# Fillers, moved steps, and the shared item and the product with V between the two banks of scores of a slot

## The chip, the cores and the metric

The kernel runs on one core of one Trainium2 chip. The metric is the device time of one execution in microseconds.

## What is computed

The input is X, 8 batches of 512 rows of 256 numbers in float32. After a layer norm, xn goes two ways: through causal attention with 16 heads of 16 and rotary positions, and through a linear layer whose input and weight are each rounded to fp8 (e4m3) with one scale for the whole tensor. Both results are added to X.

```python
Q, K, V = xn @ W_q.T, xn @ W_k.T, xn @ W_v.T           # split into 16 heads of 16
scores = rope(Q) @ rope(K).T * 16 ** -0.5              # causal: later keys masked
heads  = softmax(scores) @ V
attn   = heads_side_by_side @ W_o.T
ffn    = fake_quant_fp8(xn) @ fake_quant_fp8(weight).T + bias
out    = X + attn + ffn
# fake_quant_fp8(t): scale = 448 / max|t|; round(t * scale to e4m3) / scale
```

## The kernel before

All work is written out by hand, engine by engine, as one loop over slots (`for slot in range(FIRST_SLOT, END_SLOT)`, slots -11 to 162) in each of the five programs. Twenty slots (`SLOTS`) make a batch of 512 rows; slot 20n + s of batch n handles unit s of its exponents, while the row maxima of the same kind of unit run ten slots ahead (`LEAD`).

In a slot TensorE computes two halves of scores (`scores`, `attend`, `compare`). A half is one bank of transposed scores for the exponent (`st_ps`, two banks, heads of one half of the rows of the array) and one bank of plain scores for the row maximum (`s_ps`, three banks). `attend` waits until the exponent two banks before has been read (`exp_done`), `compare` until the row maximum three banks before has (`max_done`). ScalarE turns each `st_ps` bank into `prob` (`exp`), GpSimd masks it (`mask`), VectorE takes the row maxima (`row_max`).

After the scores TensorE does the slot's shared item, if it has one, in one of two banks `m_ps` that the items take by turns: a projection of Q or K (`qk`, read by VectorE's `rope`), of V (`v`, read by ScalarE's `copy_v` in the slot after), a turn of the row maxima (`mt`, read by VectorE's `split_max`, whose result goes by DMA into the rows of Q), a turn of the heads (`o`, read by VectorE's `norm`), a turn of the normed attention (`at`, read by ScalarE's `copy_at`), an output block (`fin`, read by VectorE's `finish`), and the two steps that spread the largest values for the fp8 scales (`spread`). `OFFSETS`, `LAST_FINS`, `EARLY` and `SPREAD` give the slots, `bank_free` waits for the reader of the item two before. Last in the slot comes the product with V (`pv`, into the one bank `o_ps`, 17 columns a head): for each group g of four heads its first block, 8 products, in slot 5g + 3 and the others, 24 products, in slot 5g + 6. The first block waits for the copy of the group before out of `o_ps` (`copy_heads`, ScalarE); the turn of heads frees `heads` for the next batch's copy.

Each engine's list of a slot, in order:

- ScalarE: `high_x` (every 20 slots), the two exponents (`exp`), `copy_turned` and `normalise` for the later batches' inputs, `copy_v`, at slot 21 the scaled weights, `qv` (scaled x for fp8), `copy_heads` of the last group (slot 22, that is 2 of the next batch), `copy_at`, `copy_heads` of the other groups (slots 7, 12, 17), `high` (half-precision part of Q and K, slots 16 and 1).
- VectorE: two banks of row maxima, `largest` (largest value of one batch, slots 0, 2, ... 14), the weight steps, `statistics` of batches 6 and 7 (slot -9), the readers of the items, the fp8 steps `qe` and `qc`.
- GpSimd: `split_x`, `mask`, `invert` of late batches, `rotate` and `low` for Q and K, the fp8 steps, the residual with the bias (`residual_at`).
- SP: all DMAs, in one list: residuals, rows of maxima, writing and reading back the split Q and K.

Ahead of the loop the inputs are normalised, batch 0 is projected (`project_whole`) and TensorE multiplies the identity by itself (`keep_busy`) between waits. In slots -10 to -3 it also turns the inputs of batches 2 to 7 (`turn_rows`).

Of the kernel before, what the change touches and what calls it, by code (L numbers as in the profile page):

```python
# [12 lines left out]
ALU = mybir.AluOpType  # L13
# [3 lines left out]
P = 128  # L17
# [37 lines left out]
LAST_FINS = {("fin", 0): 29, ("fin", 1): 30, ("fin", 2): 34, ("fin", 3): 35}  # L55
SPREAD = [(17, "spread", 0, 0), (19, "spread", 0, 1)]
# [7 lines left out]
TURN_SLOT = {2: -10, 3: -8, 4: -7, 5: -6, 6: -4, 7: -3}  # L64
DVE_STATS, ACT_STATS = (0, 1, 2, 3, 6, 7), (4, 5)


def schedule():
# [6 lines left out]
    items += [(slot, len(order), kind, n, k) for slot, kind, n, k in SPREAD]  # L75
    return [(slot, kind, n, k) for slot, _, kind, n, k in sorted(items) if n < NB - 1 or kind not in ("o", "at", "fin")]
# [39 lines left out]
def residual_at(slot, loop, last):  # L116

    for n in range(NB):
        if slot == SLOTS * n + (loop if n < NB - 1 else last):
            return n  # L120
    return None
# [5 lines left out]
def quant_at(slot, step):  # L127

    k = QUANT_STEPS.index(step)
    first, last, loop = (24, 25, 26, 27, 29), (8, 9, 12, 13, 15), (11, 13, 14, 24, 26)  # L130
    return [n for n in range(NB) if SLOTS * n + (first if n == 0 else last if n == NB - 1 else loop)[k] == slot]
# [17 lines left out]
def attention_ffn_block(nc, x, wq, wk, wv, wo, wf, bias, cos, sin, out):  # L149
    with ExitStack() as ctx:  # L150
# [303 lines left out]
        def _(eng):  # L454
# [81 lines left out]
            for slot in range(FIRST_SLOT, END_SLOT):  # L536
# [9 lines left out]
                if slot == -LEAD + 2:  # L546
                    invert(6)
                    invert(7)
# [4 lines left out]
                if slot == 23:  # L553
# [13 lines left out]
                n = residual_at(slot, 31, 17)  # L567
# [7 lines left out]
        def _(eng):  # L575
# [33 lines left out]
            def weight_step(s):  # L609
# [6 lines left out]
                if s == 15:  # L616
# [3 lines left out]
                if s == 17:  # L620
# [4 lines left out]
                    eng.tensor_scalar(amax_d[:, :], ident[0:2, 0:2], amax_r[:, 0:1], None, ALU.mult)\  # L625
                       .then_inc(wquant, 1)
                if s == 19:
# [5 lines left out]
                    eng.tensor_scalar(unscale[:, :], amax_b[:, :], 1.0 / FP8_MAX, None, ALU.mult).then_inc(wquant, 1)  # L633
                    eng.wait_ge(wquant, 5)
                    eng.tensor_scalar(scale[:, :], inv[:, :], FP8_MAX, None, ALU.mult).then_inc(wquant, 1)
# [3 lines left out]
                if s == 22:  # L639
# [100 lines left out]
            for slot in range(FIRST_SLOT, END_SLOT):  # L740
# [5 lines left out]
                if slot in range(0, 2 * NB, 2):  # L746
                    largest(slot // 2)
                weight_step(slot)
                if slot == -LEAD + 1:
                    statistics(6, 7)  # L750
# [17 lines left out]
        def _(eng):  # L768
# [96 lines left out]
            for slot in range(FIRST_SLOT, END_SLOT):  # L865
# [6 lines left out]
                if n is not None:  # L872
                    high_x(n)
                at = exponent_slot(slot)
# [6 lines left out]
                for n, i in [(n, i) for _, n, i in shared_at(slot - 1, "v")]:  # L881
                    copy_v(n, i, shared["v", n, i])
                if slot == 21:
                    eng.wait_ge(wquant, 7)
                    eng.mul(qv[:, 0:nw], wf_sb[:, :, :].rearrange("p c n -> p (c n)"), scale[:, 1:2])\
                       .then_inc(wf_scaled, 1)
                    eng.mul(wo_sb[:, :, :], wo_sb[:, :, :], scale[:, 0:1]).then_inc(wo_scaled, 1)
# [9 lines left out]
                n = batch_at(slot, 22)  # L897
                if n is not None:
                    copy_heads(n, NG - 1)
# [15 lines left out]
        def _(eng):  # L915
            eng.wait_ge(consts, 6)

            def keep_busy(count):

                for _ in range(count):  # L920
                    eng.matmul(s_ps[2][:, 0:P], ident[:, :], ident[:, :], start=True, stop=True)  # L921
# [68 lines left out]
            def scores(at, ahead):  # L990


                for half in range(2):
                    for i in range(2):
                        if at is not None and i < len(unit_parts(at[1] % 5, half)):
                            attend(*at, half, i)
                        if ahead is not None and i < len(MAX_BANKS[(2 * ahead[1] + half) % len(MAX_BANKS)]):
                            compare(ahead[0], 2 * ahead[1] + half, i)
# [89 lines left out]
            def bank_free(item):  # L1088
# [3 lines left out]
                if at >= 2:  # L1092
# [3 lines left out]
                    else:  # L1096
# [19 lines left out]
            keep_busy(24)  # L1116
# [65 lines left out]
```

## Time and profile before

| | us |
|---|---|
| time, median of 3 runs | 442.33 |
| lowest and highest of them | 439.71, 443.72 |
| the profiled execution | 441.93 |
| its span in the profile | 440.2 |
| TensorE busy | 392.0 |
| VectorE busy | 355.9 |
| ScalarE busy | 300.0 |
| GpSimd busy | 247.5 |

Busy time counts an engine's instructions with overlaps taken out once. A matmul's end is modelled, so a busy TensorE need not run at its peak. The granted clock is the share of full speed that TensorE was given; it has two levels here, 0.5 (1.2 GHz) and 1.0 (2.4 GHz).

### The profile page before, as it was taken

What the parts mean: (1) busy time and instruction counts of PE and PEld (TensorE: products, weight loads), DVE (VectorE), ACT (ScalarE), POOL (GpSimd) and SP (SyncE); (2) the same over time, 40 slices, a digit from 0 to 9 for tenths busy, and PEclk for the clock granted to TensorE, in tenths of its full rate; (3) what the DMA queues carried; (4) which work ended last, traced back from release to release, by engine and by line L of the source; (5) the groups of instructions that cost most, each with busy time, mean ns of one, the idle gap of its engine ahead of it and who ended that gap; (6) DMA issues with size and microseconds to landing.
All of it is one profiled execution on the core that took longest, in us unless ns stands there. A gap on an engine that the chain in (4) does not pass through costs nothing.

```text
span 440.2 us, 9436 instructions
## 1 busy us (share of the span) xinstructions
PE 392.0 (89%) x2986; PEld 206.8 (47%) x2986; DVE 355.9 (81%) x1360; ACT 300.0 (68%) x505; POOL 247.5 (56%) x270
## 2 busy tenths in 40 slices
PE   7997988989669999899989998999899988985976
PEld 6684652434224545454445444544454443442325
DVE  4869749798886999799979997999799978992104
ACT  3697736456566778677867786778677777765451
POOL 5555502343366857775777577757676745364360
PEclk9999575698578999999999999999999999999689
DMA  8962223000421115412441234123413431110111
GB/s 280 305 167 49 85 85 74 1 3 1 133 85 39 37 47 137 123 37 59 126 120 39 73 110 122 38 87 109 109 38 100 109 95 39 49 36 18 48 50 48
DMA packets 27810, 36.40 MB, mean 83 GB/s; under 512 B 3984, under 2 KB 25872, under 8 KB 26320
## 3 DMA queue, kind: packets, MB, share of 16 engines
q1 hardware_dynamic: 27760, 35.79, 28.9%
q8 instruction: 24, 0.39, 0.4%
q14 instruction: 26, 0.21, 0.2%
HBM read 22.94 MB, written 12.58 MB: 81 GB/s over the span
## 4 chain that ended last, share of the span: by engine, by line
PE 64%; DVE 17%; ACT 7%; issue 7%; POOL 2%; DMA 1%; DVEq 0%; ACTq 0%; POOLq 0%
PE o_ps L1075 15%; PE st_ps L965 10%; PE m_ps L1006 8%; DVE scratch L658 7%; PE m_ps L949 7%; PE s_ps L984 7%; PE m_ps L1033 7%; ACT prob L818 5%; DVE prod L606 3%; PE m_ps L1013 2%; PE s_ps L921 2%; PE m_ps L1041 1%; DVE prod L605 1%; PE m_ps L1053 1%; PE st_ps L929 1%
## 5 line engine op out<-in xcount | busy, mean ns | idle before, releaser
L818 ACT ACTIVATE prob<-st_ps,exp_scale 128x512 f32<-128x512 f32 x320 | 204.5, 688 | 96.6 <-PE st_ps L965 95.7
L658 DVE CUSTOM_DVE_ANT_0 scratch<-s_ps,causal 128x512 bf16<-128x512 f32 (+3 forms) x512 | 220.9, 483 | 34.2 <-PE s_ps L984 33.2
L511 POOL TENSOR_SCALAR_AFFINE_SELECT prob<-prob 128x512 f32<-128x512 f32 (+1 forms) x160 | 88.0, 551 | 156.0 <-ACT prob L818 154.2
L984 PE MATMUL s_ps<-k_st,q_st 48*128 48x512 f16 (+3 forms) x512 | 112.2, 319 | 13.2 <-DVE rowmax L658 13.1
L965 PE MATMUL st_ps<-q_st,k_st 50*128 50x128 f16 (+3 forms) x512 | 110.4, 316 | 12.6 <-ACT prob L818 11.0
L1075 PE MATMUL o_ps<-prob,v_sb 128*17 128x512 f32 (+3 forms) x1024 | 90.6, 476 | 6.9 <-ACT heads L832 5.1
L965 PEld LDWEIGHTS st_ps<-q_st,k_st 50*128 50x128 f16 x512 | 34.7, 96 | 98.2 <-ACT prob L818 71.2
L984 PEld LDWEIGHTS s_ps<-k_st,q_st 48*128 48x128 f16 x512 | 34.4, 96 | 30.4 <-DVE rowmax L658 22.0
L658 DVE DVE_READ_ACCUMULATOR2_ANT rowmax<- 128x1 f32 x512 | 41.0, 80 | 0.0
L1075 PEld LDWEIGHTS o_ps<-prob,v_sb 128*17 128x17 f32 x1024 | 24.4, 102 | 34.6 <-issue 20.3
L1006 PE MATMUL m_ps<-wv_sb,xnT 128*128 128x256 f32 x128 | 34.8, 419 | 0.0
L1033 PE MATMUL m_ps<-wo_sb,attnT 128*128 128x256 f32 x116 | 32.7, 404 | 0.0
L346 POOL TENSOR_TENSOR parts<-rot,parts 128x1024 f16<-128x1024 f32 x14 | 30.1, 2152 | 4.5 <-ACT parts L803 4.5
L1006 PEld LDWEIGHTS m_ps<-wv_sb,xnT 128*128 128x128 f32 x128 | 24.7, 203 | 7.2 <-issue 4.1
L605 DVE SCALAR_TENSOR_TENSOR prod<-m_ps,qk_scale,cos_sb 128x512 f32<-128x512 f32 x30 | 22.3, 742 | 7.0 <-PE m_ps L949 5.2
L679 DVE SCALAR_TENSOR_TENSOR x_res<-m_ps,both,x_res 128x256 f32<-128x256 f32 x29 | 13.9, 479 | 17.2 <-PE m_ps L1041 10.0
L832 ACT COPY heads<-o_ps 128x512 f32<-128x512 f32 x32 | 18.8, 588 | 11.7 <-PE m_ps L1013 8.3
L949 PE MATMUL m_ps<-x_parts,wk_parts 128*128 128x512 f32 x84 | 23.4, 413 | 0.0
L1033 PEld LDWEIGHTS m_ps<-wo_sb,attnT 128*128 128x128 f32 x116 | 19.6, 189 | 7.7 <-issue 6.2
L949 PE MATMUL m_ps<-x_parts,wq_parts 128*128 128x512 f32 x84 | 22.9, 410 | 0.0
L1013 PE MATMUL m_ps<-ident,heads 128*128 128x128 f32 x116 | 19.5, 292 | 3.5 <-DVE attn L671 3.4
L606 DVE SCALAR_TENSOR_TENSOR prod<-m_ps,qk_scale,sin_sb 128x512 f32<-128x512 f32 x30 | 22.1, 736 | 0.0
(123 smaller groups left out, 497.3 us busy)
## 6 DMA issues: line engine op xcount, KB each, us to landing
qk_parts<-parts SPq DMA_DIRECT2D x14, 512.0 KB, 3.1
xnT<-x_dram SPq DMA_DIRECT2D x8, 512.0 KB, 8.4
x_res<-x_dram SPq DMA_DIRECT2D x8, 512.0 KB, 5.1
q_st<-qk_parts SPq DMA_DIRECT2D x15, 256.0 KB, 4.5
k_st<-qk_parts SPq DMA_DIRECT2D x15, 256.0 KB, 3.7
out_dram<-x_res SPq DMA_DIRECT2D x7, 512.0 KB, 3.7
q_st<-qk_parts SPq DMA_DIRECT2D x17, 128.0 KB, 3.6
k_st<-qk_parts SPq DMA_DIRECT2D x17, 128.0 KB, 4.1
```

The source lines that it names most:

```text
L346: eng.tensor_tensor(parts[:, w, 1, a:z, :], rot[:, w, a:z], parts[:, w, 0, a:z, :], ALU.subtract).then_inc(low_done[w], z - a)
L511: eng.affine_select(out=ap, in_=ap, compare_op=ALU.is_ge, fill=0.0, base=0, pattern=pat, channel_multiplier=-1).then_inc(masked, 1)
L606: eng.scalar_tensor_tensor(out=c, in0=bank[:, :], scalar=to_range, in1=sin_sb[:, :], op0=ALU.mult, op1=ALU.mult)\
L658: eng.tensor_tensor_reduce(scratch[:, at % 3, col:col + w], s_ps[at % 3][:, col:col + w], causal[:, T - w:T], 1.0, NEG, ALU.add, ALU.max, ...
L818: eng.activation(prob[u][:, half * T:(half + 1) * T], st_ps[ST_BANK[2 * s + half]][:, :], ACT.Exp, scale=exp_scale[:, 0:1]).then_inc(exp_d ...
L949: mm = eng.matmul(bank[:, :], w_parts[k // 2][:, wp, c, k % 2, :], x_parts[:, xp, c, :], start=(i == 0), stop=(i == len(terms) - 1))
L965: mm = eng.matmul(st_ps[ST_BANK[i]][:, col:col + T - kb * P], k_rows(n, h, ROWS + SHIFT, slice(kb * P, (kb + 1) * P)), q_rows(n, h, ROWS + ...
L984: mm = eng.matmul(s_ps[(BANKS * n + f) % 3][:, col:col + (qb + 1) * P], q_rows(n, h, ROWS, slice(qb * P, (qb + 1) * P)), k_rows(n, h, ROWS ...
L1006: mm = eng.matmul(bank[:, t * D:(t + 1) * D], xnT[:, n, c, (2 * i + t) * P:(2 * i + t + 1) * P], wv_sb[:, c, :], start=(c == 0), stop=(c = ...
L1013: mm = eng.transpose(bank[:, g * P:(g + 1) * P], heads[:, g, qb * P:(qb + 1) * P], ident[:, :])
L1033: mm = eng.matmul(bank[:, 0:D], attnT[:, qb, c, :], wo_sb[:, c, :], start=(first and c == 0), stop=(not first and c == NC - 1))
L1075: mm = eng.matmul(o_ps[32 * i:32 * i + VW, kb * P:T], v_sb[:, n % 2, kb, g * HG + i, :], prob[u][:, col:col + T - kb * P], start=(kb == 0) ...
```

## The change

The diff does these things:

- TensorE: the two halves of scores are called apart. The first half, then `turn_rows`, fillers, the shared item and the product with V, then the second half.
- Fillers: 6 products of the identity in each of slots -10 to -1 (`FILL`, into `st_ps[1]`), and 8 in each of slots 0, 2, 4, 5, 7, 20, 22, 25 (`BUSY`), which take a turn among the shared items' banks. A wait for the weights' range (`w_max_done`) comes ahead of the loop, as `st_ps[1]` was read for it.
- ScalarE: `copy_heads` of the last group and `copy_v` come ahead of the slot's exponents. The other copies of heads stay behind them.
- VectorE: `largest` in slots 0, 2, 4, 5, 7, 8, 9, 11; `statistics` of batch 6 in slot -10, of 7 in slot -7; the weight steps one or two slots earlier; three operations on a few numbers in another form (`amax_d`, `unscale`, `scale`).
- GpSimd: `invert` of batch 6 in slot -9 and of 7 in -6; the weight's last fp8 steps a slot earlier; the residual of batch 6 in slot 148 instead of 151.
- The first two output blocks of batch 6 in slots 151 and 152 instead of 149 and 150; batch 0's fp8 steps a slot later; the two spread steps two slots earlier.

```diff
-LAST_FINS = {("fin", 0): 29, ("fin", 1): 30, ("fin", 2): 34, ("fin", 3): 35}
-SPREAD = [(17, "spread", 0, 0), (19, "spread", 0, 1)]
+LAST_FINS = {("fin", 0): 31, ("fin", 1): 32, ("fin", 2): 34, ("fin", 3): 35}
+SPREAD = [(15, "spread", 0, 0), (17, "spread", 0, 1)]
...
+FILL = {slot: 6 for slot in range(-LEAD, 0)}
+BUSY = {slot: 8 for slot in (0, 2, 4, 5, 7, 20, 22, 25)}
+LARGEST_SLOT = (0, 2, 4, 5, 7, 8, 9, 11)
...
+    items += [(slot, len(order), "busy", slot, count) for slot, count in BUSY.items()]
...
-def residual_at(slot, loop, last):
+def residual_at(slot, loop, last, last_but_one=None):
...
-        if slot == SLOTS * n + (loop if n < NB - 1 else last):
+        if slot == SLOTS * n + (last if n == NB - 1 else last_but_one or loop if n == NB - 2 else loop):
...
-    first, last, loop = (24, 25, 26, 27, 29), (8, 9, 12, 13, 15), (11, 13, 14, 24, 26)
+    first, last, loop = (25, 26, 27, 28, 30), (8, 9, 12, 13, 15), (11, 13, 14, 24, 26)
...
-                if slot == -LEAD + 2:
+                if slot == -LEAD + 1:
                     invert(6)
+                if slot == -LEAD + 4:
                     invert(7)
...
-                if slot == 23:
+                if slot == 22:
                     eng.wait_ge(wquant, 8)
...
-                n = residual_at(slot, 31, 17)
+                n = residual_at(slot, 31, 17, 28)
...
-                if s == 15:
+                if s == 13:
                     eng.wait_ge(amax_done, NB + 1)
...
-                if s == 17:
+                if s == 15:
...
-                    eng.tensor_scalar(amax_d[:, :], ident[0:2, 0:2], amax_r[:, 0:1], None, ALU.mult)\
+                    eng.tensor_tensor(amax_d[:, :], ident[0:2, 0:2], amax_r[:, 0:1].to_broadcast([2, 2]), ALU.mult)\
                        .then_inc(wquant, 1)
-                if s == 19:
+                if s == 17:
...
-                    eng.tensor_scalar(unscale[:, :], amax_b[:, :], 1.0 / FP8_MAX, None, ALU.mult).then_inc(wquant, 1)
+                    eng.tensor_scalar(unscale[:, :], shared["spread", 0, 1][:, 0:2], 1e-12, 1.0 / FP8_MAX, ALU.max, ALU.mult)\
+                       .then_inc(wquant, 1)
...
-                    eng.tensor_scalar(scale[:, :], inv[:, :], FP8_MAX, None, ALU.mult).then_inc(wquant, 1)
+                    eng.scalar_tensor_tensor(out=scale[:, :], in0=inv[:, :], scalar=FP8_MAX, in1=inv[:, :], op0=ALU.mult,
+                                             op1=ALU.max).then_inc(wquant, 1)
...
-                if s == 22:
+                if s == 21:
...
-                if slot in range(0, 2 * NB, 2):
-                    largest(slot // 2)
+                if slot in LARGEST_SLOT:
+                    largest(LARGEST_SLOT.index(slot))
                 weight_step(slot)
-                if slot == -LEAD + 1:
-                    statistics(6, 7)
+                if slot in (-LEAD, -LEAD + 3):
+                    statistics(6 if slot == -LEAD else 7)
...
+                n = batch_at(slot, 22)
+                if n is not None:
+                    copy_heads(n, NG - 1)
+                for n, i in [(n, i) for _, n, i in shared_at(slot - 1, "v")]:
+                    copy_v(n, i, shared["v", n, i])
                 at = exponent_slot(slot)
                 if at is not None:
                     exp(*at)
...
-                for n, i in [(n, i) for _, n, i in shared_at(slot - 1, "v")]:
-                    copy_v(n, i, shared["v", n, i])
-                if slot == 21:
+                if slot == 19:
...
+                if slot == 20:
                     eng.mul(wo_sb[:, :, :], wo_sb[:, :, :], scale[:, 0:1]).then_inc(wo_scaled, 1)
...
-                n = batch_at(slot, 22)
-                if n is not None:
-                    copy_heads(n, NG - 1)
...
-            def keep_busy(count):
+            def keep_busy(count, bank=s_ps[2]):
...
-                    eng.matmul(s_ps[2][:, 0:P], ident[:, :], ident[:, :], start=True, stop=True)
+                    eng.matmul(bank[:, 0:P], ident[:, :], ident[:, :], start=True, stop=True)
...
-            def scores(at, ahead):
-
-
-                for half in range(2):
-                    for i in range(2):
...
+            def scores(at, ahead, half):
+
+
+                for i in range(2):
...
-                    else:
+                    elif kind != "busy":
...
+            eng.wait_ge(w_max_done, 4)
...
-                scores(exponent_slot(slot), maximum_slot(slot))
+                scores(exponent_slot(slot), maximum_slot(slot), 0)
                 for n in [n for n, at_slot in TURN_SLOT.items() if at_slot == slot]:
                     turn_rows(n)
-                for item in shared_at(slot, *do):
+                if slot in FILL:
+                    keep_busy(FILL[slot], st_ps[1])
+                for item in shared_at(slot, "busy", *do):
                     bank_free(item)
+                    if item[0] == "busy":
+                        keep_busy(item[2], shared[item])
+                        continue
                     do[item[0]](item[1], item[2], shared[item]).then_inc(full[item[0]], 1)
...
+                scores(exponent_slot(slot), maximum_slot(slot), 1)
```

## Rows read from the trace of the kernel before

**Rows 1.** The page's first part: busy us (share of the span) xinstructions.

```profile
PE 392.0 (89%) x2986; PEld 206.8 (47%) x2986; DVE 355.9 (81%) x1360; ACT 300.0 (68%) x505; POOL 247.5 (56%) x270
```

**Rows 2.** Busy time by stretch; columns: stretch, us, busy per engine, PEclk, DMA, GB/s.

```profile
33.90:63.00 29.10, 26.61 (x110) 16.64 (x109) 21.67 (x93) 17.04 (x32) 12.38 (x12) 0.71 0.29 79
...
63.60:116.40 52.80, 43.58 (x284) 17.97 (x282) 48.28 (x162) 32.50 (x52) 20.15 (x27) 0.76 0.18 44
116.40:165.30 48.90, 42.84 (x328) 20.25 (x328) 41.55 (x161) 33.80 (x54) 30.51 (x32) 0.87 0.18 48
165.30:208.70 43.40, 41.24 (x349) 21.44 (x349) 40.36 (x159) 32.94 (x53) 29.48 (x31) 1.00 0.32 87
```

**Rows 3.** The same view of three stretches at the lower clock.

```profile
43.70:60.80 17.10, 17.01 (x61) 10.50 (x61) 10.40 (x44) 9.22 (x18) 6.87 (x5) 0.50 0.36 109
67.60:84.70 17.10, 15.25 (x88) 4.16 (x89) 15.74 (x56) 9.91 (x17) 6.29 (x8) 0.50 0.24 48
...
405.60:415.80 10.20, 8.73 (x49) 2.86 (x49) 2.54 (x6) 3.50 (x6) 3.41 (x4) 0.50 0.16 52
```

**Rows 4.** Timeline, slots 40 and 50 to 51: start us, us, engine line op out<-in.

```profile
165.22 1.13 PE L1033 MATMUL m_ps<-wo_sb,attnT 128*128 128x256 f32 x4
166.50 0.39 PE L965 MATMUL st_ps<-q_st,k_st 50*128 50x512 f16 x1
...
185.70 0.39 PE L965 MATMUL st_ps<-q_st,k_st 50*128 50x512 f16 x1
186.19 1.27 ACT L818 ACTIVATE prob<-st_ps,exp_scale 128x512 f32<-128x512 f32 x2 [1.20 <-PE st_ps L965]
186.24 1.67 PE L949 MATMUL m_ps<-x_parts,wq_parts 128*128 128x512 f32 x6
186.34 0.69 DVE L658 CUSTOM_DVE_ANT_0 scratch<-s_ps,causal 128x512 bf16<-128x512 f32 x1 [1.03 <-PE s_ps L984]
188.59 1.49 PE L1075 MATMUL o_ps<-prob,v_sb 128*17 128x384 f32 x24
```

**Rows 5.** Timeline of ScalarE in slots 41 and 42.

```profile
168.14 1.04 ACT L803 CAST parts<-rot 128x1024 f16<-128x1024 f32 x1
169.15 1.27 ACT L818 ACTIVATE prob<-st_ps,exp_scale 128x512 f32<-128x512 f32 x2
170.31 0.59 ACT L832 COPY heads<-o_ps 128x512 f32<-128x512 f32 x1
```

**Rows 6.** Timeline of TensorE in slot 48, the wait before each in brackets.

```profile
180.86 0.66 PE L1013 MATMUL m_ps<-ident,heads 128*128 128x128 f32 x4 [0.49 <-DVE attn L671]
...
182.25 1.05 PE L1075 MATMUL o_ps<-prob,v_sb 128*17 128x512 f32 x8 [0.73 <-ACT heads L832]
```

**Rows 7.** Timeline of slots 51 to 53.

```profile
189.49 1.15 ACT L895 ACTIVATE qv<-xnT,scale 128x1024 f32<-128x1024 f32 x1
...
191.67 0.60 ACT L832 COPY heads<-o_ps 128x512 f32<-128x512 f32 x1
...
193.26 1.05 PE L1075 MATMUL o_ps<-prob,v_sb 128*17 128x512 f32 x8
```

**Rows 8.** Timeline ahead of the loop: 24 fillers, two records each.

```profile
25.60 5.62 PE L921 MATMUL s_ps<-ident 128*128 128x128 f32 x48 [0.68 <-DVE parts L346]
```

**Rows 9.** Timeline of the weight steps in slots 17 and 19, and GpSimd beside them.

```profile
107.83 2.13 POOL L346 TENSOR_TENSOR parts<-rot,parts 128x1024 f16<-128x1024 f32 x1
...
108.06 1.93 DVE L625 TENSOR_SCALAR amax_d<-ident,amax_r 2x2 f32<-2x2 f32 x1
...
113.90 0.14 DVE L629 TENSOR_SCALAR amax_b<-m_ps 128x2 f32<-128x2 f32 x1
...
115.26 1.19 DVE L635 TENSOR_SCALAR scale<-inv 128x2 f32<-128x2 f32 x1
```

**Rows 10.** Timeline of slot 151: the residual of batch 6 and TensorE's wait.

```profile
403.67 2.34 POOL L570 TENSOR_TENSOR x_res<-x_res,bias_sb 128x1024 f32<-128x1024 f32 x1
...
406.66 0.38 PE L1053 MATMUL m_ps<-ident,rowmax 128*16 128x128 f32 x1 [4.68 <-DVE x_res L679]
```

More of the change, by code:

```diff
@@ L988, in compare @@
                     mm.then_inc(s_full, 1)
-            def scores(at, ahead):
-                for half in range(2):
-                    for i in range(2):
[L995 to L998, printed above, removed]
+            def scores(at, ahead, half):
+                for i in range(2):
+                    if at is not None and i < len(unit_parts(at[1] % 5, half)):
+                        attend(*at, half, i)
+                    if ahead is not None and i < len(MAX_BANKS[(2 * ahead[1] + half) % len(MAX_BANKS)]):
+                        compare(ahead[0], 2 * ahead[1] + half, i)
             def project_v(n, i, bank):
```

## The prediction

> **What bounds the kernel now.** I read the page's header first, then the busy times by stage, then the order of time in single slots. A slot here is one step of the loop; slot 0 is the first with an exponent, twenty slots make a batch. On the page TensorE is busy 89% of the span, VectorE 81% [rows 1], which says little, since the stages are not alike [rows 2]. A steady batch (165.3 to 208.7 us) takes 43.4 us with TensorE busy 41.24 and VectorE 40.36, at a granted clock of 1.00: TensorE sets the pace and has only 2.2 us of idle time to give back. Batch 0 (63.6 to 116.4 us) takes 52.8 us with VectorE busy 48.28 and TensorE at a granted clock of 0.76: there VectorE is nearly the bound. Batch 1 takes 48.9 us, TensorE busy 42.84 at 0.87. The ten slots ahead of batch 0 take 29.1 us, TensorE busy 26.61 at 0.71.
>
> The two longest slow stretches differ too [rows 3]: in 43.7 to 60.8 us TensorE at 0.50 is busy 17.01 of 17.1 us, so the clock costs time; in 67.6 to 84.7 us VectorE is busy 15.74 of 17.1 us, so a faster TensorE gives little.
>
> **Fillers ahead of slot 0.** Ten slots get 6 identity products each. 48 records, two to a product, take 5.62 us at full clock [rows 8], so one product costs 0.234 us and sixty cost 14.0 us. The stretch's own TensorE work at full clock is 26.61 less half of the 17.01 us spent at 0.50, so 18.1 us. Together 32.1 us, all in program order, against 29.1 now: **+3.0 us**, though the clock stays up. If these fillers ran at 1.2 GHz instead they would cost 28 us; if they only filled waits, nothing. I take full speed, because the first dense run of them in the trace is at full speed. The statistics of batches 6 and 7 are split over two slots; that removes VectorE's longest block here but is hidden once TensorE is the bound.
>
> **Batch 0.** Five slots get 8 fillers, 40 x 0.234 = 9.4 us. TensorE spends 0.24 / 0.5 = 48% of 52.8 us at half speed, 25 us, about 0.85 busy; at full speed it needs 43.6 - 10.7 = 33, with fillers 42, with the waits below about 46. VectorE needs 48.3 less what the three small operations with a new form give back. The one on amax_d took 1.93 us for 2x2 numbers and ended as GpSimd's 2.13 us operation beside it ended; scale took 1.19, and I take 1.1 for unscale, while amax_b, read from PSUM, took 0.14 [rows 9]. At 0.14 us each 3.8 us go, so VectorE's bound lies between 44.5 and 48.3. I take 47 plus 2 of idle time, 49: **-3.8 us**. The largest-value reductions keep their number and only move.
>
> The Trainium skill ("SBUF — State Buffer", Who interferes with whom) says that a VectorE instruction with two SBUF inputs also contends with a GpSimd instruction that reads SBUF. By it the new forms for amax_d and scale would still be held and only unscale, which now reads PSUM, would go free: 1.0 us instead of 3.8. The row of amax_d agrees with its general rule that one of the two blocks for a whole instruction.
>
> **Batch 1.** Three slots get 8 fillers, 5.6 us. TensorE's busy time at full clock is 42.84 less half of 12.7 us, 36.5; with fillers 42.1, with the waits of the next part (some 5.4, slot 25's late scaling of x among them) 47.5 against 48.9: **-1.4 us**. The weight steps, one or two slots earlier, and batch 0's first scaling, one later, lie beside this work.
>
> **The new order within a slot.** Before, TensorE's list reads: both halves of scores, then the shared item, then the product with V. After: first half, item, product, second half. Since the second half of slot s is followed at once by the first of slot s+1, the scores still come as bursts of two, 0.54 us each [rows 4], with the same columns. No TensorE work is saved. What changes is which results stand in line. ScalarE's list is still exponent, exponent, then copies; the second exponent now can't begin before the slot's item and product are done, so every copy behind it comes later against TensorE, and the next slot's first exponent stands behind those copies. So do the VectorE readers of an item, behind the second row maximum.
>
> From [rows 4]: a burst's first exponent starts 0.49 us after the burst, its row maximum 0.64 us after. From [rows 5]: two exponents take 1.16 us from start to next operation, 0.58 each; one runs 0.69. In the new order the burst holds the second half of s and the first of s+1, and between their exponents lie the copies c. The attention scores of the next burst's second part need that exponent, at 0.49 + 0.58 + c + 0.69 = 1.76 + c, and stand 0.23 into the burst at 0.54 + mid + 0.23. The wait is 1.0 + c - mid, where mid is the work between.
>
> - Slot 2: c is the half-precision copy, 168.14 to 169.15, and the copy of heads, 0.59 [rows 5], 1.6 us; mid is one output block, 165.22 to 166.50, 1.28 us [rows 4]. Wait 1.3 us.
> - Slots 6 and 7: high_x, a copy of 1024 columns like the 1.0 us one, before the exponent, mid 1.6 (the 24 products of [rows 4], 1.49, and a turn of maxima): 0.4. Then the turn of attn waits for the split of the row maxima, which now stands behind the later row maximum; 0.4 more. Together 0.8.
> - Slot 8: already the turn of heads waits 0.49 us for VectorE's norm and the product with V 0.73 us for the copy of heads [rows 6]. The norm comes 0.64 us and a row maximum (0.69) and its own two operations (I take 0.7) after the burst, 2.0 in all, and its bank is wanted after 0.54: 1.4 instead of 0.49, 0.9 more.
> - Slots 12 and 13: the scaled x, 1.15 us [rows 7] (mid is the projection of [rows 4], 1.67 with its overlap), 0.5; and the copy of heads. Now it starts at 191.67 and the product needs it at 193.26 [rows 7]; in the new order it ends 0.49 + 0.58 + 0.59 = 1.7 us after the burst, wanted after 0.54 and a turn of some 0.6. With the first wait counted, 0.8 in all.
> - Slots 17 and 18: the other half-precision copy, 0.4, and the copy of heads wanted right after the burst: 1.3 in all.
>
> The sum is 5.1 us per batch. Waits of this size give VectorE time to catch up, so the rest of the present 2.2 us of idle time beside slot 8's 1.2, about 1.0, goes: **+4.0 us** per steady batch. The bounds: 0, if the copies find room that I don't see, and 5.5. Four such batches give +16. Batch 6 has no projections behind it and waits for ScalarE anyway: +3. The first half of batch 7 has slots 7 and 8 and little else: +2. What of this is hidden: nothing, as TensorE is busy 41.24 of 43.4 us and everything else follows its list. The copies of V and of the last group of heads are put ahead of the exponents, which I counted; the other three copies of heads are left where they were. SP's list, with all DMA issues, is unchanged.
>
> **The end.** The output blocks of batch 6 stand in slots 149 and 150 but need the residual that GpSimd adds in slot 151: it starts at 403.67, and TensorE stands still 4.68 us for the bank, until 406.66 [rows 10]. After, GpSimd adds in slot 148 and the blocks come at 151 and 152. The standstill goes, and with it some of the cost of the 10.2 us at 0.50 that begin at 405.6 us [rows 3], of which I take 2.5. New waits of the kind above cost 1.2 here: **-6 us**.
>
> **The sum.** +3.0 - 3.8 - 1.4 + 16 + 3 + 2 - 6 = +12.8 us on the profiled execution's 441.93 us (span 440.2): 454.7, so 455. The median of the runs, 442.33, is 0.4 above that execution, so the same number stands.
>
> **Rivals.**
> 1. The new order costs nothing, because the copies and readers keep up with TensorE. Then what is left is the fillers, the clock and the end: +3.0 - 3.8 - 1.4 - 7.2 = -9.4, so 433 us. For it: ScalarE is busy only 32.94 of 43.4 us. Against: its slack lies at the wrong places; in [rows 6] the product with V waits for the copy of heads already. It decides below 9.4 / 5.8 = 1.6 us of new waits per batch. Chance 0.13.
> 2. The waits are about half of mine, two a batch: near 443 us. Chance 0.11.
> 3. The fillers don't hold the clock, or batches 0 and 1 gain nothing: 14 us more for the sixty, so 469 us. For it: TensorE busy all through 43.7 to 60.8 us did not raise it. Against: little there was a dense 128x128 product, and the clock rose after the projections of V began. Chance 0.08.
> 4. The clock alone decides: the granted clocks of [rows 2] mean 16.9 + 25.3 + 12.7 = 54.9 us at half speed in the first three stages, all won back at half their length, with the new order free: 27.5 less, 414.4 us. Against it is VectorE's 15.74 of 17.1 us. Chance 0.02.
>
> The fourth is what the Trainium skill makes of it ("TensorE: Matmul & The Clock Gate", Terms): the penalty of throttled time is that time by one minus the granted share. By this trace it holds for 43.7 to 60.8 us at most.
>
> **The numbers.** My own case has 0.66: 455, from 446 to 465. The rivals below it reach down to 433 and further, the third up to 469. The range 438 to 468 leaves out about 2 in 10. About 1% is what a measurement can tell. Slower by over 1% (above 446.7): my case nearly whole and the third, 0.74; within 1%: the second, 0.11; faster: the first, the fourth, 0.15.
>
> **What would show it.** Right: a steady batch of 47 to 48 us at full clock; waits of the product with V for the copy of heads at three slots of each batch, where now it is slot 8 alone; a wait of the attention scores for the exponent at slot 2; no 4.7 us standstill near the end; the clock at 1.0 through slots -10 to 8; slot 0 later than now. Wrong: a steady batch still at 43.4 us would leave rival 1; a clock at 0.50 before slot 0 would be rival 3; batches 0 and 1 well under 47 us would mean that I took VectorE's bound too high.

## The result and the profile after

| | before | after |
|---|---|---|
| median us | 442.9 (439.7 to 443.7) | 481.5 (479.0 to 484.8) |
| ratio | 1 | 1.091, 95% interval 1.084 to 1.098 |
| the profiled execution | 441.93 | 479.31 |
| its span | 440.2 | 477.6 |

The change makes the kernel 9% slower. The forecast was slower by 13 us, 455 us in all; the measured loss is 37 us between the profiled executions and 39 us between the medians, and 481.5 us lies outside the range of 438 to 468.

The page after, first the busy times, then the clock in 40 slices, in tenths of full speed:

```profile
PE 413.4 (87%) x3234; PEld 230.7 (48%) x3234; DVE 355.7 (74%) x1360; ACT 301.4 (63%) x505; POOL 250.5 (52%) x270
...
PEclk9999999999999998999889998999799979996977
```

VectorE, ScalarE and GpSimd work as long as before, within 3 us ([rows 1]); TensorE has 248 records more, the fillers. The clock now stays up until 187 us. Then it falls to 0.5 for a short while in every batch, which it never did in the steady batches (2 to 5) before. The busy times by stretch (columns as in [rows 2]: the stretch, its us, busy time of each engine, granted clock, DMA). The stretches are batches 1, 2, 3 and 6; the last line is one of the falls, in batch 3:

```profile
116.20:167.40 51.20, 44.18 (x380) 24.13 (x379) 41.55 (x163) 35.86 (x57) 32.61 (x33) 1.00 0.25 65
167.40:216.50 49.10, 43.20 (x350) 21.82 (x348) 40.60 (x159) 33.12 (x53) 30.02 (x31) 0.97 0.29 77
216.50:267.00 50.50, 44.58 (x350) 22.17 (x348) 40.66 (x159) 33.14 (x53) 30.08 (x31) 0.93 0.27 75
...
366.50:414.90 48.40, 38.51 (x326) 18.04 (x324) 35.14 (x151) 31.08 (x51) 22.62 (x27) 0.93 0.30 82
...
235.10:241.90 6.80, 6.22 (x23) 3.06 (x23) 1.98 (x8) 2.39 (x4) 2.24 (x2) 0.50 0.36 81
```

A steady batch went from 43.4 us to 49.1 or 50.5; TensorE's idle time in it from 2.2 us to 5.9. Batch 1 went from 48.9 [rows 2] to 51.2 although the clock rose from 0.87 to 1.00. Laid out by the start of the first exponent of each stage, in the profiled executions:

| stage | before | after | forecast change | change |
|---|---|---|---|---|
| start to slot 0 | 63.5 | 66.4 | +3.0 | +2.9 |
| batch 0 | 50.3 | 49.8 | -3.8 | -0.5 |
| batch 1 | 51.4 | 50.8 | -1.4 | -0.6 |
| batches 2 to 5 | 174.0 | 199.1 | +16 | +25.1 |
| batch 6 | 39.9 | 48.4 | +3 | +8.5 |
| slots 140 to 149 | 20.8 | 24.3 | +2 | +3.5 |
| slot 150 to the end | 40.4 | 38.8 | -6 | -1.6 |

(The split between batches 0 and 1 depends on the marks. By the stretches of [rows 2], which begin and end at TensorE's work, batch 0 won 3.5 us and batch 1 lost 2.3. By either the two together won 1.1 or 1.2 us where 5.2 were forecast.)

Whom TensorE waits for, in the whole program (us in total, times, longest us). The first line is from the kernel before, the others from the changed one:

```profile
PE o_ps L1075 <- ACT heads L832: 5.1, 7, 0.7
...
PE st_ps L973 <- ACT prob L825: 16.5, 33, 1.2
PE o_ps L1082 <- ACT heads L839: 14.6, 18, 1.1
PE m_ps L1020 <- DVE attn L678: 9.5, 7, 1.4
PE o_ps L1082 <- POOL prob L515: 4.5, 7, 0.8
PE m_ps L1027 <- DVE shift L700: 3.6, 7, 0.8
```

The waits for the exponent (`prob`, ScalarE) come first. Next is the copy of heads: 18 waits where there were 7, one a batch, as in [rows 6]. The waits for `attn` are slot 8, those for `shift` slot 7. The waits for a mask (`prob` by GpSimd), 7 where the kernel before has one, stood in no step of the forecast.

How slot 82 (slot 2 of batch 4) now runs, ScalarE and TensorE in order of time:

```profile
270.55 1.04 ACT L810 CAST parts<-rot 128x1024 f16<-128x1024 f32 x1
271.49 0.59 ACT L839 COPY heads<-o_ps 128x512 f32<-128x512 f32 x1
271.96 1.93 ACT L825 ACTIVATE prob<-st_ps,exp_scale 128x512 f32<-128x512 f32 x3
...
272.72 0.23 PE L973 MATMUL st_ps<-q_st,k_st 50*128 50x128 f16 x1 [0.97 <-ACT prob L825]
```

Against [rows 5]: the same two copies, but now they lie between the second exponent of slot 81 and the first of slot 82, and TensorE's scores for slot 83 wait for the latter. TensorE in slots 87 and 88:

```profile
282.28 0.66 PE L1027 MATMUL m_ps<-ident,attn 128*128 128x128 f32 x4 [0.51 <-DVE shift L700]
...
284.83 0.66 PE L1020 MATMUL m_ps<-ident,heads 128*128 128x128 f32 x4 [1.35 <-DVE attn L678]
286.22 1.89 PE L1082 MATMUL o_ps<-prob,v_sb 128*17 128x512 f32 x8 [0.73 <-ACT heads L839]
```

In [rows 6] the last two waits were 0.49 and 0.73 us. And the eight products of the last line run 1.89 us where they ran 1.05: the clock has just fallen (at 286.3 us).

### The profile page after: what moved, and what is told of

It is laid out like the page before. It is cut to its first block, busy times and chain, and to the rows that moved or that the text cites. A ratio compares the mean times of both kernels' runs of the same rounds, so it can differ in the third digit from the quotient of the medians.

```text
span 477.6 us, 9930 instructions
## 1 busy us (share of the span) xinstructions
PE 413.4 (87%) x3234; PEld 230.7 (48%) x3234; DVE 355.7 (74%) x1360; ACT 301.4 (63%) x505; POOL 250.5 (52%) x270
## 4 chain that ended last, share of the span: by engine, by line
PE 58%; DVE 16%; ACT 12%; issue 9%; POOL 3%; DMA 1%; DVEq 0%; ACTq 0%; POOLq 0%
PE o_ps L1082 13%; PE st_ps L973 7%; PE m_ps L1013 7%; DVE scratch L665 7%; PE m_ps L957 6%; PE s_ps L992 5%; ACT prob L825 5%; PE m_ps L1040 4%; ACT heads L839 3%; PE st_ps L929 3%; PE m_ps L929 3%; PE m_ps L1020 2%; ACT qv L906 1%; PE s_ps L929 1%; DVE prod L611 1%
## 5 line engine op out<-in xcount | busy, mean ns | idle before, releaser
L825 ACT ACTIVATE prob<-st_ps,exp_scale 128x512 f32<-128x512 f32 x320 | 210.5, 690 | 128.0 <-PE st_ps L973 126.7
L665 DVE CUSTOM_DVE_ANT_0 scratch<-s_ps,causal 128x512 bf16<-128x512 f32 (+3 forms) x512 | 226.5, 482 | 77.1 <-PE s_ps L992 76.0
L515 POOL TENSOR_SCALAR_AFFINE_SELECT prob<-prob 128x512 f32<-128x512 f32 (+1 forms) x160 | 92.8, 582 | 186.7 <-ACT prob L825 186.7
L973 PE MATMUL st_ps<-q_st,k_st 50*128 50x128 f16 (+3 forms) x512 | 107.3, 309 | 19.7 <-ACT prob L825 16.5
L992 PE MATMUL s_ps<-k_st,q_st 48*128 48x512 f16 (+3 forms) x512 | 105.8, 307 | 0.0
L1082 PE MATMUL o_ps<-prob,v_sb 128*17 128x512 f32 (+3 forms) x1024 | 87.4, 461 | 19.7 <-ACT heads L839 14.6
L1082 PEld LDWEIGHTS o_ps<-prob,v_sb 128*17 128x17 f32 x1024 | 23.4, 98 | 46.6 <-ACT heads L839 21.5
L1013 PE MATMUL m_ps<-wv_sb,xnT 128*128 128x256 f32 x128 | 37.7, 445 | 0.0
L1013 PEld LDWEIGHTS m_ps<-wv_sb,xnT 128*128 128x128 f32 x128 | 27.0, 223 | 7.8 <-issue 3.9
L780 ACT ACTIVATE xnT<-xnT,shift_x,rstd 128x256 f32<-128x256 f32 x32 | 16.6, 596 | 9.8 <-POOL shift_x L485 9.8
```

The source lines that it names most:

```text
L515: eng.affine_select(out=ap, in_=ap, compare_op=ALU.is_ge, fill=0.0, base=0, pattern=pat, channel_multiplier=-1).then_inc(masked, 1)
L665: eng.tensor_tensor_reduce(scratch[:, at % 3, col:col + w], s_ps[at % 3][:, col:col + w], causal[:, T - w:T], 1.0, NEG, ALU.add, ALU.max, ...
L825: eng.activation(prob[u][:, half * T:(half + 1) * T], st_ps[ST_BANK[2 * s + half]][:, :], ACT.Exp, scale=exp_scale[:, 0:1]).then_inc(exp_d ...
L973: mm = eng.matmul(st_ps[ST_BANK[i]][:, col:col + T - kb * P], k_rows(n, h, ROWS + SHIFT, slice(kb * P, (kb + 1) * P)), q_rows(n, h, ROWS + ...
L992: mm = eng.matmul(s_ps[(BANKS * n + f) % 3][:, col:col + (qb + 1) * P], q_rows(n, h, ROWS, slice(qb * P, (qb + 1) * P)), k_rows(n, h, ROWS ...
L1013: mm = eng.matmul(bank[:, t * D:(t + 1) * D], xnT[:, n, c, (2 * i + t) * P:(2 * i + t + 1) * P], wv_sb[:, c, :], start=(c == 0), stop=(c = ...
```

## The experiments

The theory: the loss comes from the order of the halves alone, because ScalarE's and VectorE's lists still have both halves ahead of what hangs on the item and the product with V. The rivals: the fillers and the moved steps make it; or the order costs something of its own whatever the other lists do. Ratios are to the kernel before, measured beside each run at a median of 442.0 to 443.8 us. Times of batches and of slot 0 are of the profiled executions, by the marks of the table above.

**The old order in the changed kernel**

```diff
                 scores(exponent_slot(slot), maximum_slot(slot), 0)
+                scores(exponent_slot(slot), maximum_slot(slot), 1)
...
-                scores(exponent_slot(slot), maximum_slot(slot), 1)
```

> The changed kernel with both halves of scores ahead of the shared item again; everything else of the change stays. If the order of the halves makes the loss, a steady batch takes 43.5 us again at full clock, slot 0 starts 3 us later than before, batch 0 takes about 49 us, the 4.7 us standstill near the end is gone, and the whole takes about 433 us. If the fillers and the moved steps make the loss, it stays above 460 us.

437.4 us, ratio 0.988 (0.981 to 0.996). Steady batches take 43.6 us and the clock stays up in them:

```profile
170.00:213.00 43.00, 40.84 (x347) 21.27 (x345) 39.79 (x158) 32.41 (x52) 29.19 (x30) 1.00 0.33 88
```

The end takes 35.8 us instead of 40.4. So the order makes 44 of the changed kernel's microseconds, and the rest of the change together wins 6 us.

**The new order in the kernel before**

The same split of `scores`, in the kernel before, with the two output blocks and the residual of batch 6 moved. As the lists read, without these TensorE's slot 151 would wait for a bank that `finish` frees, `finish` for the residual, the residual for the mask of slot 151 and the mask for scores that now stand behind the wait.

> The kernel before with TensorE's new order of halves, and with the two late output blocks and the residual of batch 6 moved as in the change, since without that the new order would wait for itself in slot 151. No fillers, no copies moved. If the order makes the loss: steady batches of 49 to 51 us, in all about 485 us. If it is the fillers: 436 us, which is the kernel before less its standstill.

487.2 us (479.5 to 487.8), so wide a spread that no ratio is given; even the fastest execution is 36 us above the kernel before. The profile is of one of 487.6 us. Its steady batches take 49.0, 50.6, 50.7 and 49.0 us, which is the theory's number without a filler in it. The two of 50.6 and 50.7 us have 3.4 us at half clock each, the two of 49.0 have none. Batch 1 took 61.1 us, part of it at half clock. In this kernel the copies of V and of the last heads, which the change moves ahead of the exponents, still stand behind them, and TensorE waits 12.4 us in all (12 times) for the copy of V, where the kernel before has no such wait:

```profile
PE m_ps L1052 <- ACT v_sb L825: 12.4, 12, 1.0
```

**ScalarE's copies between the two exponents**

```diff
                 if at is not None:
-                    exp(*at)
+                    exp(*at, 0)
...
+                if at is not None:
+                    exp(*at, 1)
```

(the second stands at the end of ScalarE's slot, behind all copies)

> The changed kernel, but ScalarE's list of a slot is first exponent, copies, second exponent, in step with TensorE's. If the late copies make most of the waits, the waits for the copy of heads at slots 13 and 18 and for the exponent at slot 2 go, those for VectorE at slots 7 and 8 stay; a steady batch takes about 46 us instead of 49.2, the whole about 455 us. If ScalarE only holds these waits by name and the slow clock or VectorE is behind them, it stays above 470 us.

469.8 us, ratio 1.060 (1.053 to 1.068): 12 us less than the changed kernel, where 26 were expected. The one steady batch without a fall of the clock takes 45.9 us, as expected; the others take 47.5 to 48.9. The waits for the copy of heads are back at 5.1 us in 7 times; those for VectorE's norm stay, 9.5 us, and so do the falls of the clock (the view of [rows 3]):

```profile
236.30:243.10 6.80, 6.20 (x23) 3.06 (x23) 1.98 (x8) 2.98 (x5) 3.54 (x3) 0.50 0.36 82
284.10:290.90 6.80, 5.72 (x23) 2.76 (x24) 2.91 (x13) 3.02 (x5) 3.54 (x3) 0.50 0.52 135
```

**And VectorE's readers between the two row maxima**

```diff
                     row_max(n, 2 * s)
-                    row_max(n, 2 * s + 1)
+                for kind, n, k in shared_at(slot, "qk", "o", "fin", "mt"):
+                    ...
+                if at is not None:
+                    row_max(at[0], 2 * at[1] + 1)
```

> As the run with the copies between the exponents, and VectorE reads the shared item between its two row maxima too. If the readers standing behind the second half were the whole of the loss, a steady batch takes 43 to 44 us and the whole 432 to 438 us, below the kernel before. If the order costs something of its own, a steady batch stays above 45 us.

448.8 us, ratio 1.014 (1.007 to 1.021). Steady batches take 45.0 to 45.1 us at full clock. Three quarters of the steady loss are gone, but 1.6 us a batch stay, so the order is not free even with both lists brought into step. Among the new waits that stay are the one for the mask behind GpSimd's rotation (0.52 us at slot 16) and the one at slot 2, where the copies now hold up the second exponent (0.68).

**VectorE's readers alone**

The same edit of VectorE's list, made alone in the changed kernel; ScalarE's list is left as it was.

> The changed kernel, but VectorE reads the shared item between its two row maxima; ScalarE's copies stay behind the second exponent. If the falls of the clock at slots 8 and 9 of the steady batches come from what TensorE does in slots 7 and 8 (waits for the split of the maxima and for the norm, turns, 17-column products), they go with the 1.5 us of waits there, and a steady batch takes about 46.5 us at full clock, the whole about 464 us. If the falls come from the waits at slots 2, 13 and 18 as well, stretches at half clock stay, steady batches take 48 us or more and the whole is above 472 us.

457.6 us, ratio 1.039 (1.030 to 1.048): 24 us faster than the changed kernel, and 6 better than expected. Four steady batches run alike, at full clock:

```profile
160.50:206.40 45.90, 41.27 (x352) 20.97 (x348) 40.67 (x159) 33.01 (x52) 29.87 (x30) 1.00 0.30 82
206.40:252.30 45.90, 41.27 (x352) 20.97 (x348) 40.69 (x159) 33.00 (x52) 29.86 (x30) 1.00 0.30 82
```

though TensorE still waits for the late copies:

```profile
PE o_ps L1083 <- ACT heads L840: 15.4, 18, 1.1
```

Put beside the previous two runs: with the copies moved and VectorE's readers left late, the clock falls in three of four steady batches; with the readers moved and the copies left late, in none; with both moved, in none. So the falls go with what piles up in slots 7 and 8. That is not the whole condition: one batch of the run with the copies between, and two of the run with the new order alone, have the same waits there (1.35 us for the norm, 0.73 for the copy) and no fall. What decides between them stays open.

**The changed kernel without fillers**

```diff
-FILL = {slot: 6 for slot in range(-LEAD, 0)}
-BUSY = {slot: 8 for slot in (0, 2, 4, 5, 7, 20, 22, 25)}
+FILL = {}
+BUSY = {}
```

> The changed kernel without any fillers. If fillers cost TensorE time without winning the clock back, this is faster than the changed kernel's 481 us; slot 0 starts at about 62 us instead of 66. If they pay for themselves, stretches at half clock come back before slot 40 and the whole is at 481 to 486 us. Steady batches stay at 49 to 50.5 us either way, since no filler stands there.

476.0 us, ratio 1.075 (1.069 to 1.082): 5.5 us faster than with them. Slot 0 comes at 59.6 us instead of 66.4, though 17 us at half clock are back ahead of 75 us. Batch 0 takes 49.4 us instead of 49.8, batch 1 52.0 instead of 50.8. Steady batches stay at 49.1 to 50.5.

**The end alone, in the kernel before**

```diff
-LAST_FINS = {("fin", 0): 29, ("fin", 1): 30, ("fin", 2): 34, ("fin", 3): 35}
+LAST_FINS = {("fin", 0): 31, ("fin", 1): 32, ("fin", 2): 34, ("fin", 3): 35}
...
-                n = residual_at(slot, 31, 17)
+                n = residual_at(slot, 31, 17, 28)
```

> The kernel before with the two output blocks of batch 6 in slots 151 and 152 and its residual in slot 148, nothing else. The standstill of 4.7 us goes, and slot 150 to the end takes 35 to 36 us instead of 40.4, as in the run with the old order: in all about 438 us. If the slow clock comes back elsewhere, less: 441 us.

437.3 us, ratio 0.989 (0.982 to 0.996). Slot 150 to the end takes 36.7 us instead of 40.4. The clock still falls there, for 3.4 and 10.2 us as before, so what this edit gives is most of the 4.7 us standstill of [rows 10] and nothing of the clock. It is 3.7 of the 6 us between the profiled executions; 3.0 more lie ahead of slot 0, where the two programs are the same (60.5 against 63.5 us), and are not the edit's.

**The old order without fillers, and with the later ones only**

> The changed kernel with the old order of halves and without fillers: what remains are the moved steps, the three small operations and the end. If the 5 us that the first two batches won in the old order came from the fillers' clock, they go back to 50 and 51 us and slot 0 to 63 us: in all about 438 us. If they came from the moved steps, slot 0 comes at 63 us, the batches stay at 48 to 49 us and the whole is at 433 us.

This is the run without any. 430.5 us, ratio 0.974 (0.967 to 0.980): the lowest median of the study. Against 437.4 with fillers, slot 0 comes 7.0 us earlier (59.6), batch 0 takes 49.4 instead of 48.3 and batch 1 47.6 instead of 49.0. So the moved steps and the end make the gain, and the fillers cost 6.9 us.

> The changed kernel with the old order and only the fillers of slots 0 to 25, none ahead of slot 0. If the sixty early ones cost 3 us and the clock is won by the later ones, slot 0 comes at 62 to 63 us and the whole takes 434 us. If the early ones keep the clock up for what follows, batch 0 takes 50 us or more and the whole 438 us.

This is the run with those of slots 0 to 25 only. 432.1 us (427.9 to 432.7), ratio 0.974 (0.967 to 0.982); against the previous run's 430.5 (429.6 to 432.9) no difference is shown. Slot 0 comes at 60.4 us, batches 0 and 1 take 49.9 and 49.2. So nearly all of the cost is that of the sixty early fillers.

**GpSimd's rotation one slot later, in the changed kernel**

```diff
-CHAIN = {("rotate", 0): -27, ...
+CHAIN = {("rotate", 0): -26, ...
```

> The changed kernel with GpSimd's first rotation of Q one slot later, in slot 14 behind that slot's mask instead of in slot 13 ahead of it. If the 0.7 to 0.8 us wait of the 24 products in slot 16, which the forecast had counted at nothing, comes from the mask standing behind the rotation, it goes in batches 0 to 5, a steady batch loses 0.6 us, and the whole is 3 to 5 us faster than 481.5. If the mask is late by its exponent alone, the wait stays and the time too.

477.8 us (474.9 to 480.3), ratio 1.081 (1.074 to 1.087), 3.8 us below the changed kernel's median. The two ranges overlap, and the steady batches tell more: 48.5 us with one fall of 3.4 us and 49.8 with 6.8, where the changed kernel has 49.1 and 50.5, so 0.6 us a batch. The wait at slot 16 is gone; GpSimd in slots 93 to 95 of the changed kernel, and TensorE in slot 96:

```profile
301.73 1.20 POOL L515 TENSOR_SCALAR_AFFINE_SELECT prob<-prob 128x512 f32<-128x512 f32 x1 [1.55 <-ACT prob L825]
302.90 1.27 POOL L343 TENSOR_TENSOR rot<-prod 128x512 f32<-128x512 f32 x1
304.13 1.28 POOL L344 TENSOR_TENSOR rot<-prod 128x512 f32<-128x512 f32 x1
305.37 1.45 POOL L515 TENSOR_SCALAR_AFFINE_SELECT prob<-prob 128x512 f32<-128x512 f32 x2
...
306.51 1.49 PE L1082 MATMUL o_ps<-prob,v_sb 128*17 128x384 f32 x24 [0.69 <-POOL prob L515]
```

With the rotation later, the same products follow the turn of the maxima at once, and in the whole program 2 waits for a mask are left of 7:

```profile
PE o_ps L1082 <- POOL prob L515: 1.0, 2, 0.8
...
309.40 0.28 PE L1060 MATMUL m_ps<-ident,rowmax 128*16 128x128 f32 x1
309.60 1.49 PE L1082 MATMUL o_ps<-prob,v_sb 128*17 128x384 f32 x24
```

**The three small operations in their old form**

> The run with the old order and no fillers (430.5 us), with the three small operations of VectorE in the form of the kernel before. If they were held by GpSimd and stood on the path, they take 1 to 2 us each again and the whole 432 to 434 us. If they are hidden or start beside no GpSimd operation in these slots, 430.5 us.

431.5 us (427.8 to 433.7), ratio 0.975 (0.969 to 0.981): no difference from 430.5. First the new forms, from the run with the old order and no fillers, with the GpSimd operation beside them:

```profile
103.20 2.14 POOL L350 TENSOR_TENSOR parts<-rot,parts 128x1024 f16<-128x1024 f32 x1
...
103.49 0.14 DVE L638 TENSOR_SCALAR unscale<-m_ps 128x2 f32<-128x2 f32 x1
103.67 1.69 DVE L641 SCALAR_TENSOR_TENSOR scale<-inv 128x2 f32<-128x2 f32 x1
```

Then the old forms, from this run:

```profile
99.73 0.22 DVE L630 TENSOR_SCALAR amax_d<-ident,amax_r 2x2 f32<-2x2 f32 x1
...
105.47 2.13 POOL L350 TENSOR_TENSOR parts<-rot,parts 128x1024 f16<-128x1024 f32 x1
...
105.76 1.86 DVE L638 TENSOR_SCALAR unscale<-amax_b 128x2 f32<-128x2 f32 x1
```

Beside that operation the new `scale` ends only with it, and so does the old `unscale`; the new `unscale`, which reads PSUM, takes 0.14 us. Old-form `amax_d` took 0.22 us instead of 1.93: two slots earlier nothing of GpSimd's ran beside it. So for `amax_d` the move did it and not the form, and for `unscale` the form did it. Together the three take 1.98 us here in the new form and 2.63 in the old, which is too little to show in the time.

**The new order at its best**

The run with copies and readers between the halves, with the rotation later and without fillers.

> The new order with copies and readers between the halves on ScalarE and VectorE, the rotation one slot later, and no fillers. Of the 1.6 us by which a batch of the run with copies and readers still exceeds 43.4, the rotation takes 0.5; the fillers cost 7 us in the old order. So 438 to 440 us, still above the old order's 430.5, if the mask and the late heads are what is left. If it comes to 431 us or less, the order itself costs nothing.

437.4 us, ratio 0.990 (0.986 to 0.994), 7 us above the same steps in the old order. Steady batches take 44.6 us against 43.6. With everything brought into step the new order still costs 1 us a batch and gains nothing that the runs show. TensorE is idle 3.2 us in such a batch, 2.2 in the old order; the waits for the exponent at slots 1, 2 and 4 (0.31, 0.67 and 0.28 us) are the largest new ones.

## Why the prediction was wrong

The direction and the mechanism were right: TensorE waits for copies and readers that now stand behind later work, at the places named. The step that failed is the new order's term. It counted waits alone, +4.0 us a steady batch, and took the granted clock to stay at 1.00; a batch lost 6.3 us, with 3.4 or 6.8 us at a clock of 0.50 in each. The terms for batch 6, for slots 140 to 149 and for the end failed in the same way, and batches 0 and 1 together were put 4 us too low.

**The fillers ahead of slot 0: the number right, in part by luck.** +3.0 forecast, +2.9 measured, with TensorE busy without a gap from 36.4 to 66.1 us. But the forecast started from one profile, in which slot 0 comes at 63.5 us; the end alone, which has the same program up to there, reaches it at 60.5. With the moved statistics and no fillers ahead of slot 0, four profiles have slot 0 at 59.5, 59.6, 59.6 and 60.4 us and a fifth at 62.2, so whether moving them wins anything is not shown. Against all of these the fillers cost 4 to 7 us of their 14. The clock was held, as forecast, and won little.

**Batch 0: by its own stretch near** (-3.5 against -3.8). VectorE is busy 44.8 us in it instead of 48.3; the forecast's lower bound was 44.5. The three small operations take 0.6 us there instead of 4.2. That part was right in size and only partly in cause, as the run with the old forms shows.

**Batch 1: sign wrong by its own stretch.** The forecast's 47.5 us had 42.1 of work and 5.4 of waits; 51.2 came. TensorE was busy 44.2 us and idle 7.0, so both terms were too small. For the work, the forecast took off half of all 12.7 us at the lower clock, though TensorE was busy for only 11.5 of them; the other 1.5 us are not explained. Among the waits are 0.78 us for a mask in slot 26 and 0.56 for one in slot 36, which no step had, and one of 1.10 us in slot 32 for a row maximum.

**The new order, +4.0 a batch: found +6.3.** TensorE's idle time place by place in the changed kernel's batch 4, less what stood at that place in batch 4 before:

| place | forecast | measured |
|---|---|---|
| slot 2, copies ahead of the exponent | 1.3 | 1.0 |
| slot 4 | 0 | 0.3 |
| slots 6 and 7, high_x and the split | 0.8 | 0.7 |
| slot 8, norm and copy of heads | 0.9 | 0.7 |
| slots 12 and 13 | 0.8 | 0.3 |
| slot 16, the mask | 0 | 0.8 |
| slots 17 and 18 | 1.3 | 0.9 |
| relief of VectorE's old waits | -1.0 | -1.1 |
| the slow clock | 0 | 1.4 for each 3.4 us |

The waits sum to 3.6 with the relief, which is near the forecast's 4.0, though only because the mask, which it had left out, made up for places that it had too high. The rest is mostly the clock, which I took to stay at full speed and said nothing of as a risk here. A batch with 3.4 us of it takes 49.1 us, one with 6.8 us 50.5; that is 1.4 us for 3.4 us at half clock, and by it a batch without any would take 47.7, +4.3 on 43.4. The 0.7 us between that and the waits' 3.6 stand in no wait that the trace shows. Over batches 2 to 5 the clock is some 8 of the 25 us. The Trainium skill ("TensorE: Matmul & The Clock Gate", Terms) puts the penalty of throttled time at that time by one minus the granted share. By it 3.4 us would cost 1.7, an estimate near this trace's 1.4, where TensorE is the bound.

In batch 0 VectorE is nearly the bound. In the run in the old order without fillers 17.1 us of it are at half clock, and VectorE is busy 45.8 of its 49.4 us, so a clock at full speed could have given back at most 3.6 us, where an estimate by that rule of the Trainium skill gives 8.5. With fillers and the clock up the batch takes 48.3 us; that pair does not price the clock by itself, since the fillers are 9.4 us of work. So the fourth rival, which won back all slow time at half its length, fell.

**The masks** were counted as hidden without being named at slot 16: after mask 13 GpSimd rotates for 2.5 us, and mask 14, now half a slot later, comes behind. One line of the forecast about GpSimd's queue would have found it.

**Batch 6, +3: found +8.5.** TensorE is idle 9.9 us in it instead of 4.8. Of these 5.1 us, 3.3 stand at slots 2, 4, 7, 8 and 18, as in a steady batch. The other 1.8 stand in the bursts of slots 10, 12, 15 and 17: I wrote that this batch waits for ScalarE anyway, but the waits there grew from 3.3 to 5.1 us. The clock is at 0.50 for 6.8 us of it, some 2.8 us at the price above, which the forecast had at nothing.

**The end, -6: found -1.6.** The standstill went: the old order gains 4.6 us there, the end alone 3.7. In the new order this stage takes 3.0 us more than in the old order (38.8 against 35.8), where I took 1.2: TensorE is idle 1.5 us more, for copies among others, and 14.9 us are at half clock instead of 10.2. The same fall that reaches into it, from 433.1 us, began in slots 140 to 149, where +2 was forecast and +3.5 found.

**The rivals.** The number of the first, that the order costs nothing (433 us), is what the old order gives (430.5 to 437.4). As an account of the changed kernel it is excluded by the runs with the old order and with the new order alone. The second took half of my waits; nearly all of them came. The third asked whether the fillers hold the clock; they do. Its other half, that batches 0 and 1 gain nothing, came nearly true (1.1 us of 5.2).

## What to carry to other kernels

If one engine's list is reordered inside a step, write out for every other list which of its entries hangs on the moved work and what stands ahead of it there; an entry behind a late one is late too. Two edits (ScalarE's and VectorE's lists) gave back 33 of the 44 us here, and the order itself was worth nothing. Fillers that hold a clock stand in program order on the engine that sets the pace: the sixty here, 14 us of work, cost some 4 to 7 us net, and the later ones won nothing that shows. A run without them belongs beside each run with them. And a sum of waits need not be the whole loss: here the clock fell too where the waits piled up, which was a third of the steady loss.

## What the runs showed of the hardware

- In the changed kernel the granted clock fell to 0.5 for 3.4 or 6.8 us in each steady batch, always while TensorE was at the turn of heads or the product with V of slot 8. In the batch shown it fell after TensorE had waited 0.51, 1.35 and 0.73 us with turns and 17-column products between. With VectorE's readers brought into step and 15.4 us of waits for the copy of heads left, it never fell in a steady batch. With the same waits in slots 7 and 8 it fell in some batches and not in others of two more runs. How much of the falls is the waits and how much the kind of work between them stays open.
- The same instructions do not get the same clock: up to slot 0 the run with the end alone has the program of the kernel before, and had 10.2 us at half clock there where the kernel before had 17.1, with slot 0 at 60.5 instead of 63.5 us. The runs without fillers in the old order, with new and old forms, share a program up to slot 0 too: 3.4 us at half clock and 59.6 us against 10.2 and 62.2. So some 3 us of a single profile's first stage are of this kind.
- A VectorE operation of 2 columns (`scale`, in the run with the old order and no fillers) took 1.69 us in the form with two SBUF inputs, beside a GpSimd operation of 2.14 us with which it ended. The Trainium skill ("SBUF — State Buffer", Who interferes with whom) says that such an operation contends with a GpSimd instruction that reads SBUF. This trace agrees, and `unscale`, read from PSUM, took 0.14 us beside the same operation. In the changed kernel the same `scale` took 0.32 us and again ended with the GpSimd operation beside it, a mask that had begun 0.32 us before it.
